# A four-layer graph network on one Trainium2 core: where ScalarE copies the spherical harmonics in the first layer's loop

## The chip, the cores and the metric

The kernel runs on one core of one Trainium2 chip. A core has five engines with a queue of instructions each: PE (TensorE, matmuls), DVE (VectorE), ACT (ScalarE), POOL (GpSimd) and SP (SyncE, which here only starts transfers). They wait for each other through semaphores. The metric is the device time of one execution in microseconds (us), the median of several runs.

## The reference, cut to what matters

A graph of 6250 nodes with 32 features and 200,000 edges goes through four layers, each after a layer norm and a ReLU, each added to its input. The change lies in the first, the harmonic layer: every edge takes the features of its source node, multiplies them with the 16 spherical harmonics of its direction, and the products are summed at the target node and multiplied with a weight matrix.

```
Y = real_sh_l3(edge_vectors)                              # [edges, 16]
msg = node_features[sources][:, :, None] * Y[:, None, :]
agg = jax.ops.segment_sum(msg, targets, num_segments=n_atoms)
out = agg.reshape(n_atoms, -1) @ W + b
```

The fourth layer needs `relu(e_feat @ en1_w.T + en1_b)` for every edge, 128 hidden units. The kernel computes these in the loop of the harmonic layer, too.

## The kernel before

Ahead of the layer the edges are sorted by target, into tiles of 128 edges that share a block of 128 target nodes. A table in HBM holds, for each node, its features already multiplied with the weights, 16 x 32 numbers a node (`harmonic_table`). So an edge's message is the sum over 16 products of a gathered row with its harmonics.

`harmonic_layer` (from L1088) walks over 404 chunks of four tiles (U = 4). A turn is Q = 4 chunks, there are 101 turns, and `each_turn` (L83) puts four turns into the body of a hardware loop and writes the rest out. Nearly every buffer exists four times, by q, the chunk's number in its turn; the harmonics in PSUM (`harm_ps`) and the edges turned over (`turned`) twice. `free`, `multiplied` and the other counters start with a lead, so that the first chunks don't wait. For chunk c:

- SP (L1127, L1128) loads the harmonics and the 32 edge features, once the sum of chunk c-4 is done (`free`). Both count on `loaded[q]`.
- POOL gathers 128 rows of 2 KB for each tile, four indirect transfers a chunk (`gather_all`, L1046), once the product of chunk c-4 is done (`multiplied`); every second chunk it copies the next indices (L1034).
- ACT, in this order: |iota - target| for four tiles, the first half of a one-hot (`one_hot_away`, L1070); a copy of the chunk's harmonics from SBUF to PSUM (L1149), after a wait for the product of chunk c-2 and one for the loads; the copy that lays the turned edge features flat in SBUF (L1151); the second half of the one-hot (L1076); then it waits for the hidden units on PE, writes their ReLU to SBUF (L1156) and starts the store to HBM (L1158).
- DVE: four products of gathered rows and harmonics, which it reads from PSUM (L1226), and one reduction over the 16 (L1232), which gives the message.
- PE, in this order: flip(c) turns the edge features over (L1175), sum(c-1) adds the messages of the chunk before at their targets with the one-hot as weights (L1194), hide(c) makes the hidden units (L1183), after the lay-flat copy of c.

An engine takes its instructions in order, so what stands behind a wait waits with it.

Of the kernel before, what the change touches and what calls it, by code (L numbers as in the profile page):

```python
# [8 lines left out]
ACT = mybir.ActivationFunctionType  # L9
# [6 lines left out]
NY = 16  # L16
# [3 lines left out]
U = 4  # L20
Q = 4
# [13 lines left out]
class Steps:  # L35
# [11 lines left out]
    def turn(self, i, each):  # L47

        return Steps(self.engine, self.sem, self.base + self.n + i * each)
# [33 lines left out]
def each_turn(engine, first, end, turn, join=JOIN):  # L83

    whole = (end - first) // join
    if whole:
        with engine.Fori(0, whole) as j:
            for x in range(join):
                turn(j * join + (first + x))
    for i in range(first + whole * join, end):  # L90
        turn(i)
# [49 lines left out]
def layernorm_root(k, act, small, squares_summed, scaled):  # L141

    act.wait_ge(squares_summed, 1)
    k.nc.scalar.activation(small[:, 1, :], small[:, 1, :], ACT.Sqrt).then_inc(scaled, 1)
# [922 lines left out]
def one_hot_away(k, s, c, hot, near):  # L1067

    for u in range(U):
        last = k.nc.scalar.activation(hot[:, u, :], k.iota[:, :], ACT.Abs, bias=k.neglo[s][:, bass.ds(c * U + u, 1)])  # L1070
    last.then_inc(near, 1)


def one_hot_of(k, hot):

    return k.nc.scalar.activation(hot[:, :, :], hot[:, :, :], ACT.Relu, bias=1.0, scale=-1.0)  # L1076
# [11 lines left out]
def harmonic_layer(k):  # L1088


    nc, s = k.nc, 1
    with ExitStack() as ctx:
# [5 lines left out]
        harm = [sb(f"h_harm{q}", [P, U, NY]) for q in range(Q)]  # L1098
# [9 lines left out]
        harm_ps = [pb(f"h_harm_ps{h}", [P, 512]) for h in range(2)]  # L1108
# [3 lines left out]
        loaded = [sem(f"h_loaded{q}") for q in range(Q)]  # L1112
        stored = [sem(f"h_stored{q}") for q in range(Q)]
        near, made, flipped, flat = sem("h_near"), sem("h_made"), sem("h_flipped"), sem("h_flat")
        hidden_done, hidden_made, multiplied, msg_made = sem("h_hid_done"), sem("h_hid_made"), sem("h_multiplied"), sem("h_msg_made")
        spread, ones_set = sem("h_spread"), sem("h_ones_set")
# [4 lines left out]
        @block.sync  # L1121
        def _(sp):
            def turn(i):
                for q in range(Q):
                    c = i * Q + q
                    sp.wait_ge(free, c + 1)
                    sp.dma_start(harm[q][:, :, :], k.harm_dram.rearrange("p (t j) -> p t j", j=NY)[:, bass.ds(c * U, U), :]).then_inc(loaded[q], 16)  # L1127
                    sp.dma_start(attr[q][:, :, :], rows[:, bass.ds(c * U, U), W_A32:W_A32 + D]).then_inc(loaded[q], 16)  # L1128

            each_turn(sp, 0, k.TURNS, turn)  # L1130
# [5 lines left out]
        @block.scalar  # L1136
        def _(act):
            for q in range(Q):
                act.sem_inc(stored[q], 16)
            act.sem_inc(flat, 1)  # L1140
            act.sem_inc(hidden_made, 1)
            def turn(i):
                for q in range(Q):
                    c = i * Q + q
                    act.wait_ge(free, c + 1)
                    one_hot_away(k, s, c, hot[q], near)
                    act.wait_ge(multiplied, c + (Q - 1))
                    act.wait_ge(loaded[q], 32 * i + 32)
                    nc.scalar.activation(harm_ps[q % 2][:, 0:U * NY], harm[q][:, :, :].rearrange("p u j -> p (u j)"), ACT.Copy).then_inc(spread, 1)  # L1149
                    act.wait_ge(flipped, c + 1)  # L1150
                    nc.scalar.activation(turned[q % 2][0:D, :], turned_ps[:, :], ACT.Copy).then_inc(flat, 1)  # L1151
                    act.wait_ge(near, c + 1)
                    one_hot_of(k, hot[q]).then_inc(made, 1)
                    act.wait_ge(hidden_done, c + 1)
                    act.wait_ge(stored[q], 16 * i + 16)
                    nc.scalar.activation(hidden[q][:, :], hidden_ps[:, :], ACT.Relu).then_inc(hidden_made, 1)  # L1156
                    act.wait_ge(hidden_made, c + 2)
                    act.dma_start(k.hid_dram[:, bass.ds(c * (U * EH), U * EH)], hidden[q][:, :]).then_inc(stored[q], 16)  # L1158

            each_turn(act, 0, k.TURNS, turn)  # L1160
            for q in range(Q):
                act.wait_ge(stored[q], 16 * (k.TURNS + 1))
            layernorm_root(k, act, small, squares_summed, scaled)
# [1303 lines left out]
```

## Time and profile before

| | us |
|---|---|
| median of 3 runs | 29608.59 |
| lowest and highest | 29582.97, 29622.8 |
| span of the profiled execution (no other time of it is shown) | 29570.9 |
| of it, from 5395 to 7779: the loop of the harmonic layer | 2384 |
| DVE busy with the products (L1226) | 1002.5 |
| DVE busy with the reductions (L1232) | 923.6 |
| ACT busy with the copies of the harmonics (L1149) | 82.6 |

The span runs from the first instruction to the last of one profiled execution. Busy time is what the instructions of a group took together; idle time before them is listed with the instruction that ended it. Matmuls are pipelined, and their ends are modelled. The fourth layer takes nearly half of the span and is not touched.

### The profile page before, as it was taken

What the parts mean: (1) busy time and instruction counts of PE and PEld (TensorE: products, weight loads), DVE (VectorE), ACT (ScalarE), POOL (GpSimd) and SP (SyncE); (2) the same over time, 40 slices, a digit from 0 to 9 for tenths busy, and PEclk for the clock granted to TensorE, in tenths of its full rate; (3) what the DMA queues carried; (4) which work ended last, traced back from release to release, by engine and by line L of the source; (5) the groups of instructions that cost most, each with busy time, mean ns of one, the idle gap of its engine ahead of it and who ended that gap; (6) DMA issues with size and microseconds to landing.
All of it is one profiled execution on the core that took longest, in us unless ns stands there. A gap on an engine that the chain in (4) does not pass through costs nothing. (4 is left out here: it accounts for less than half of the span.)

```text
span 29570.9 us, 552018 instructions
## 1 busy us (share of the span) xinstructions
PE 19304.6 (65%) x125786; PEld 16885.8 (57%) x125787; DVE 14123.3 (48%) x37141; ACT 10123.7 (34%) x24027; POOL 19962.3 (68%) x21448
## 2 busy tenths in 40 slices
PE   0000610788766677733333499899899899899899
PEld 0000300566422277633333389899899899899898
DVE  7700321688788855422222244444444444444444
ACT  0000000355333354333333344444344444344444
POOL 0776775466566677577777677677677677677676
PEclk9999755555699966655555599999899999999999
DMA  2114114788411144311211222222222222222222
GB/s 95 31 29 32 27 29 101 224 240 240 130 25 25 26 125 125 93 26 26 26 26 26 34 71 67 62 70 67 62 69 67 63 69 67 64 68 66 65 69 60
DMA packets 3128329, 2133.91 MB, mean 72 GB/s; under 512 B 2037459, under 2 KB 2626549, under 8 KB 3116567
## 3 DMA queue, kind: packets, MB, share of 16 engines
q1 hardware_dynamic: 2279528, 1072.10, 15.8%
q0 software_dynamic: 736448, 837.95, 12.4%
q10 hardware_dynamic: 109680, 190.99, 1.7%
q8 instruction: 1339, 21.94, 0.3%
q14 instruction: 1334, 10.93, 0.1%
HBM read 1679.95 MB, written 419.35 MB: 71 GB/s over the span
## 5 line engine op out<-in xcount | busy, mean ns | idle before, releaser
L2057 POOL DMA_INDIRECT e_got<-round_table,e_ring x9384 | 8984.7, 957 | 3690.5 <-issue 3047.8
L2278 DVE SCALAR_TENSOR_TENSOR e_spread<-e_ring,e_nodes,e_got 128x128 f32 x18816 | 5561.1, 352 | 6145.2 <-PE e_outer_ps L2177 3385.4
L2177 PE MATMUL e_outer_ps<-e_ring,e_spread 128*128 x37632 | 5530.2, 292 | 1153.8 <-issue 664.6
L2177 PEld LDWEIGHTS e_outer_ps<-e_ring,e_spread 128*128 128x128 f32 x37632 | 4843.2, 201 | 1273.6 <-issue 1273.6
L2085 ACT ACTIVATE e_outer<-e_outer_ps 128x516 f32<-128x516 f32 x4704 | 2824.1, 600 | 7278.5 <-PE e_outer_ps L2177 7144.6
L2198 PE MATMUL e_sum_ps<-w,e_turned 128*128 128x32 f32 x37632 | 4550.8, 273 | 0.0
L2198 PEld LDWEIGHTS e_sum_ps<-w,e_turned 128*128 128x128 f32 x37632 | 4476.2, 193 | 115.9 <-issue 115.9
L1046 POOL DMA_INDIRECT g_got<-second_table,g_index x3232 | 3082.5, 954 | 931.5 <-issue 741.0
L1871 PE MATMUL g_sums<-g_load,g_hot 128*128 128x64 f32 x6464 | 1566.4, 424 | 2562.1 <-DVEq L1903 2541.2
L1871 PEld LDWEIGHTS g_sums<-g_load,g_hot 128*128 128x128 f32 x6464 | 1438.6, 327 | 2689.8 <-issue 2668.5
L2188 PE MATMUL e_turn_ps<-ident,e_outer 128*128 128x128 f32 x18816 | 2926.6, 280 | 0.0
L2096 ACT ACTIVATE e_turned<-e_turn_ps 128x512 f32<-128x512 f32 x4704 | 2786.2, 592 | 33.0 <-PE e_turn_ps L2188 25.7
L2188 PEld LDWEIGHTS e_turn_ps<-ident,e_outer 128*128 128x128 f32 x18816 | 2307.5, 146 | 0.0
L1357 PE MATMUL m_spread<-m_diag,m_hot 128*128 128x512 f32 x3232 | 1666.7, 642 | 806.5 <-DVE m_diag L1373 806.4
L1046 POOL DMA_INDIRECT m_got<-near_table,m_index x1616 | 1529.3, 946 | 863.3 <-issue 583.0
L1046 POOL DMA_INDIRECT h_got<-harmonic_table,h_index x1616 | 1532.0, 948 | 783.6 <-issue 439.0
L740 POOL DMA_INDIRECT edges_by_src<-s_rows,s_to x1563 | 1600.8, 1024 | 610.6 <-issue 473.2
L1500 POOL DMA_INDIRECT edges_by_node<-a_inner x1616 | 1552.3, 961 | 531.0 <-issue 462.6
L1070 ACT ACTIVATE g_hot<-iota,neglo 128x128 f32<-128x128 f32 x3232 | 1031.3, 389 | 2482.8 <-PE g_sums L1871 2480.8
L740 POOL DMA_INDIRECT edges_by_dst<-s_rows,s_to x1563 | 1500.7, 960 | 486.7 <-issue 474.2
L765 ACT ACTIVATE s_rows<-words 128x44 f32 (+2 forms) x286 | 68.3, 239 | 4759.5 <-DMA edges_by_src<-s_rows,s_to 2124.3
L1357 PEld LDWEIGHTS m_spread<-m_diag,m_hot 128*128 128x128 f32 x3232 | 577.9, 198 | 1894.6 <-DVE m_diag L1373 1452.1
(393 smaller groups left out, 22752.2 us busy)
## 6 DMA issues: line engine op xcount, KB each, us to landing
e_ring<-edges_by_node SPq DMA_DIRECT2D x2346, 272.0 KB
e_got<-round_table,e_ring POOLq DMA_INDIRECT x9384
edge_hidden<-h_hidden ACTq DMA_DIRECT2D x404, 256.0 KB, 3.8
a_inner<-edge_hidden SPq DMA_DIRECT2D x404, 256.0 KB
g_got<-second_table,g_index POOLq DMA_INDIRECT x3232, 2.4
s_rows<-edge_attr SPq DMA_DIRECT2D x284, 176.0 KB, 2.7
edges_by_src<-pad ACTq DMA_DIRECT2D x16, 2020.0 KB, 35.0
edges_by_dst<-pad ACTq DMA_DIRECT2D x16, 2020.0 KB, 51.4
```

The source lines that it names most:

```text
L740: g.indirect_dma_start(k.edges[s], bass.IndirectOffsetOnAxis(ap=to[h][0:parts, u:u + 1], axis=0), rows[h][0:parts, u, :], None).then_inc(s ...
L1046: g.indirect_dma_start(into[q][:, u, :], None, table, bass.IndirectOffsetOnAxis(ap=index[q // 2][:, at:at + 1], axis=0)).then_inc(landed[q ...
L1357: last = nc.tensor.matmul(spread_ps[h][:, u, :], hot[q][:, h * HALF + u, :], diag[q % 2 * PAIRS + h][:, u, :, :].rearrange("p h e -> p (h ...
L1500: g_.indirect_dma_start(k.fine_rows, bass.IndirectOffsetOnAxis(ap=to, axis=0), inner[q][:, u, :], None).then_inc(scattered[q], 16)
L1871: last = nc.tensor.matmul(sums[q % 2][:, u * W:(u + 1) * W], hot[q][:, u, :], load[q][:, u, :], start=True, stop=True)
L2057: g_.indirect_dma_start(got[:, u, :], None, k.round_table, bass.IndirectOffsetOnAxis(ap=index, axis=0)).then_inc(landed[q], 16)
L2085: a_.activation(outer[h][:, at:at + U, :], outer_ps[:, n % 2 * 1024:(n % 2 + 1) * 1024].rearrange("p (x f) -> p x f", x=U)[:, :, 0:FULL], ...
L2096: a_.activation(turned[h][:, :, at:at + U * NEAR], turn_ps[:, n % 2 * 512:(n % 2 + 1) * 512].rearrange("p (x i) -> p i x", i=D), ACT.Copy) ...
L2177: last = t_.matmul(outer_ps[:, to:to + FULL], spread[n % 4][:, x, :], ring[:, bass.ds(at[x], 1), 0:FULL].rearrange("p a f -> p (a f)"), st ...
L2188: last = t_.transpose(turn_ps[:, to:to + P], outer[h][:, n % EACH * U + x, 0:P], k.ident[:, :])
L2198: t_.matmul(msg_ps, turned[h][:, i, :], k.w2[:, i * D:(i + 1) * D], start=i == 0, stop=False)
L2278: last = v.scalar_tensor_tensor(spread[n % 4][:, x, :].rearrange("p (j i) -> p j i", j=NEAR), ends.unsqueeze(2).to_broadcast(wide), nodes[ ...
```

## The change

ScalarE copies the harmonics one chunk ahead: those of chunk 0 before the loop, those of chunk c+1 between the second half of the one-hot of c and the wait for the hidden units of c. The two waits of the copy move with it. The number of copies and the buffers are the same. The last turn is written out on its own, because its last chunk has no next one.

```diff
-            def turn(i):
+
+            def show_harmonics(i, q):
+
+                act.wait_ge(multiplied, i * Q + (q + Q - 1))
+                act.wait_ge(loaded[q], 32 * i + 32)
+                nc.scalar.activation(harm_ps[q % 2][:, 0:U * NY], harm[q][:, :, :].rearrange("p u j -> p (u j)"), ACT.Copy).then_inc(spread, 1)
+
+            def turn(i, last=False):
                 for q in range(Q):
                     c = i * Q + q
                     act.wait_ge(free, c + 1)
                     one_hot_away(k, s, c, hot[q], near)
-                    act.wait_ge(multiplied, c + (Q - 1))
-                    act.wait_ge(loaded[q], 32 * i + 32)
-                    nc.scalar.activation(harm_ps[q % 2][:, 0:U * NY], harm[q][:, :, :].rearrange("p u j -> p (u j)"), ACT.Copy).then_inc(spread, 1)
                     act.wait_ge(flipped, c + 1)
                     nc.scalar.activation(turned[q % 2][0:D, :], turned_ps[:, :], ACT.Copy).then_inc(flat, 1)
                     act.wait_ge(near, c + 1)
                     one_hot_of(k, hot[q]).then_inc(made, 1)
+                    if not (last and q == Q - 1):
+                        show_harmonics(*((i, q + 1) if q < Q - 1 else (i + 1, 0)))
                     act.wait_ge(hidden_done, c + 1)
                     act.wait_ge(stored[q], 16 * i + 16)
                     nc.scalar.activation(hidden[q][:, :], hidden_ps[:, :], ACT.Relu).then_inc(hidden_made, 1)
...
-            each_turn(act, 0, k.TURNS, turn)
+            show_harmonics(0, 0)
+            each_turn(act, 0, k.TURNS - 1, turn)
+            turn(k.TURNS - 1, last=True)
```

## Rows read from the trace of the kernel before

**Rows 1.** Windows: start:end, length, busy us of each engine, clock, DMA share, GB/s

```profile
5395.00:7779.00 2384.00, 1971.09 (x8078) 1608.54 (x8077) 1923.76 (x2019) 1216.80 (x3227) 1571.58 (x1818) 0.50 0.83 239
5402.00:5452.00 50.00, 38.18 (x158) 31.59 (x159) 40.78 (x45) 23.52 (x63) 38.78 (x45) 0.51 0.89 263
7780.00:9000.00 1220.00, 805.02 (x1648) 296.74 (x1649) 1017.46 (x1698) 368.84 (x959) 743.42 (x865) 0.93 0.13 24
```

**Rows 2.** Waits, 5390 to 7790: who waited for whom, us, times, longest

```profile
ACT h_hidden L1156 <- PE h_hidden_ps L1183: 877.8, 404, 6.5
...
DVE h_product L1226 <- ACT h_harm_ps L1149: 438.3, 402, 6.3
PE h_sums L1194 <- DVE h_msg L1232: 397.4, 401, 5.8
...
DVE h_product L1226 <- DMA h_got<-harmonic_table,h_index: 9.1, 2, 8.0
```

**Rows 3.** Time line, two chunks: start, us, engine, line, operation, idle before

```profile
6511.23 2.48 DVE L1226 TENSOR_TENSOR h_product<-h_got,h_harm_ps 128x512 f32<-128x512 f32 x4 [0.63 <-ACT h_harm_ps L1149]
...
6513.75 2.29 DVE L1232 TENSOR_REDUCE h_msg<-h_product 128x128 f32<-128x2048 f32 x1
...
6516.18 1.91 PE L1194 MATMUL h_sums<-h_msg,h_hot 128*128 128x32 f32 x8 [0.56 <-DVE h_msg L1232]
...
6517.12 0.20 ACT L1149 ACTIVATE h_harm_ps<-h_harm 128x64 f32<-128x64 f32 x1
6517.27 0.57 ACT L1151 ACTIVATE h_turned<-h_turned_ps 32x512 f32<-32x512 f32 x1
6517.46 2.48 DVE L1226 TENSOR_TENSOR h_product<-h_got,h_harm_ps 128x512 f32<-128x512 f32 x4 [1.43 <-ACT h_harm_ps L1149]
6517.75 0.61 ACT L1076 ACTIVATE h_hot<-h_hot 128x512 f32<-128x512 f32 x1
...
6518.02 2.07 PE L1183 MATMUL h_hidden_ps<-en,h_turned 33*128 33x128 f32 x8
...
6518.79 0.38 SPq L1128 DMA_DIRECT2D h_attr<-edges_by_dst  x1
...
6520.02 1.03 PE L1175 MATMUL h_turned_ps<-ident,h_attr 128*32 128x128 f32 x4
6520.13 0.60 ACT L1156 ACTIVATE h_hidden<-h_hidden_ps 128x512 f32<-128x512 f32 x1 [1.77 <-PE h_hidden_ps L1183]
...
6521.38 1.28 ACT L1070 ACTIVATE h_hot<-iota,neglo 128x128 f32<-128x128 f32 x4 [0.65 <-ACT h_hidden L1156]
...
6522.56 0.20 ACT L1149 ACTIVATE h_harm_ps<-h_harm 128x64 f32<-128x64 f32 x1
...
6522.89 2.48 DVE L1226 TENSOR_TENSOR h_product<-h_got,h_harm_ps 128x512 f32<-128x512 f32 x4 [0.63 <-ACT h_harm_ps L1149]
```

**Rows 4.** Tile h_harm_ps: count, ns min/median/max, first and last start

```profile
L1226 DVE TENSOR_TENSOR h_product<-h_got,h_harm_ps x1616: 678/681/690, 5402.0 to 7778.4; 128x512 f32<-128x512 f32 x180
L1149 ACT ACTIVATE h_harm_ps<-h_harm x404: 202/204/228, 5395.8 to 7776.3; 128x64 f32<-128x64 f32 x135
```

**Rows 5.** Time line at a turn of ScalarE's loop

```profile
6715.86 1.28 ACT L1070 ACTIVATE h_hot<-iota,neglo 128x128 f32<-128x128 f32 x4 [1.05 <-issue]
...
6717.19 0.57 ACT L1151 ACTIVATE h_turned<-h_turned_ps 32x512 f32<-32x512 f32 x1
...
6717.81 2.07 PE L1183 MATMUL h_hidden_ps<-en,h_turned 33*128 33x128 f32 x8 [0.20 <-ACT h_turned L1151]
...
6720.01 0.60 ACT L1156 ACTIVATE h_hidden<-h_hidden_ps 128x512 f32<-128x512 f32 x1 [1.73 <-PE h_hidden_ps L1183]
```

**Rows 6.** Groups of POOL, 5390 to 7790: busy us, mean ns, idle before

```profile
L1046 POOL DMA_INDIRECT h_got<-harmonic_table,h_index x1616 | 1532.0, 948 | 783.6 <-issue 439.0 <-DVE h_product L1226 291.5 <-DMA h_got<-harmonic_table,h_index 50.3
L1034 POOL COPY h_index<-other 128x8 int32 (+1 forms) x203 | 40.8, 201 | 50.4 <-POOLq L965 36.1 <-issue 13.9
```

**Rows 7.** Tile h_attr, from issue to landing

```profile
DMA to landing us min/median/max: 2.7/3.7/11.7
```

## The prediction

> **What bounds the kernel now.** The page puts the harmonic layer in one stretch of 2384 us, and only this stretch is touched. I read its engine shares first, then who waits for whom, then the time line of two chunks, and last the engines' own work as floors.
>
> In the stretch no engine is full: PE is busy 1971 us (83%), DVE 1924 (81%), POOL 1572 (66%, without the time between its instructions), ACT 1217 (51%), and the 16 DMA engines 83%; PE runs at a granted clock of 0.50, that is 1.2 GHz [rows 1]. So the stage is bound by a round of waits, not by an engine. The waits say which: DVE's product waits for ScalarE's copy of the harmonics in 402 of 404 chunks, 438 us in all; PE's summing waits 397 us for DVE's message; ScalarE waits 878 us for the hidden units on PE [rows 2]. These three make one circle. The copy of the harmonics needs nothing of PE, but in ScalarE's program it stands behind the wait for the hidden units of the chunk before.
>
> The time line shows one lap [rows 3]. Call the chunk whose product starts at 6511.23 n. Product to reduction 2.52 us (6511.23 to 6513.75), the reduction 2.29, then 0.14 until PE starts to sum n (6516.18). From there: 1.84 to hide(n+1) at 6518.02, 2.11 to ScalarE's ReLU of it at 6520.13, 1.25 to the one-hot's first half for n+2 (6521.38; in it lie the ReLU's 0.60 and the issue of its store), 1.18 to the copy of the harmonics of n+2 (6522.56), and 0.33 to the product of n+2 (6522.89). Together 2.52 + 2.29 + 0.14 + 1.84 + 2.11 + 1.25 + 1.18 + 0.33 = 11.66 us for two chunks, which is what lies between the two products. Chunk n+1 (product at 6517.46) runs the same lap, shifted. So the steady period is **5.83 us a chunk**. The mean over the layer is (7776.3 - 5395.8)/403 = 5.91 [rows 4]; the 0.08 between them are the opening, a few late transfers, and ScalarE's loop turn every 16 chunks, whose gap before the one-hot is 1.05 in place of 0.65 [rows 5]. These I leave as they are.
>
> **The change part by part.**
>
> 1. The copy of chunk c+1 now stands in front of the wait for hide(c). Number and size of the copies are the same: 404 of 0.20 us, so added work is nothing, and each moves past no DMA of its own queue except the store of the hidden units, which it now precedes. ScalarE gets there with time to spare: between the one-hot's second half (6517.75 + 0.61 = 6518.36) and the ReLU (6520.13) it sits idle 1.77 us [rows 3], and the copy takes 0.20 of them. That is its cover. In the new pace below the same gap is 1.7 us, so it stays covered; without that cover it would cost up to 0.20 x 404 = 81 us. The last lap's circle is opened: the product of c+1 no longer hangs on hide(c).
>
> 2. Between the one-hot's first half and the lay-flat copy the harmonics are gone: 6517.12 to 6517.27, 0.15 us a chunk [rows 3].
>
> 3. Two waits come forward with the copy: for product(c-1), which frees the PSUM bank, and for the loads of chunk c+1. Behind them on ScalarE stand the ReLU, its store and the next one-hot, and PE waits for those. What they cost in the new pace is worked out below: nothing, with room.
>
> 4. The first copy ahead of the loop waits for a load that the old code waited for as well; the gather of chunk 0 sets the first product at 5402.0 [rows 4], long after the copy. Nothing. The last turn was written out before too (101 turns are 25 times 4 and one), so there is no code more to load.
>
> **What is late next.** With this circle open, each remaining one has a period of its own, and the longest sets the pace:
>
> - ScalarE and PE: hide(c), ReLU(c), one-hot(c+1), lay-flat(c+1), hide(c+1). When PE really waits for the lay-flat copy, as it does once at a loop turn, hide starts 0.62 after the copy's start (6717.19 to 6717.81) and the ReLU starts 2.20 after hide (6720.01) [rows 5]. With 1.25 and 1.18 from [rows 3] that is 2.20 + 1.25 + 1.18 + 0.62 = **5.25 us**. With the 2.11 of an unhindered PE it would be 5.16.
> - POOL: its 1616 gathers are busy 1532.0, idle 783.6, of which 291.5 only for DVE's product, and its index copies take 40.8 plus the 14 of issue before them: (1532.0 + 783.6 - 291.5 + 40.8 + 14)/404 = 5.15 at most [rows 6].
> - DVE: 2.52 + 2.29 = 4.81, some 0.1 more to start the next product.
> - PE alone: summing 1.84, hide 2.00 (6518.02 to 6520.02), flip 1.03: 4.87 [rows 3].
> - DMA: 0.83 of 2384/404 = 5.90 is 4.90 us a chunk at a share of one [rows 1].
>
> I take 5.25, because it is the longest and comes from a place where exactly this wait was the last. Is nothing else in its way? Count from the start of hide(c) as t. The second half of the one-hot ends at about t + 0.45, the copy for c+1 runs to t + 0.65, and the ReLU is due at t + 2.20. Product(c+1) can start at t + 0.8, product(c) a period earlier, so its reduction ends near t + 0.4; PE wants it after the flip, at t + 3.0. Product(c-1) ended still earlier, so the wait for the bank costs nothing. The loads of c+1 are issued when sum(c-3) ends, just ahead of hide(c-2), at t - 10.5; the second is issued 0.8 later (6518.79 against 6518.02 [rows 3]) and lands in 3.7 (median), at t - 6.0; even the slowest, 11.7 [rows 7], is there at t + 2.0, ahead of the ReLU. POOL starts the gather for c+4 when product(c) has ended and has over 10 us until it is needed.
>
> **The sum.** (5.83 - 5.25) x 404 = 234 us less in the layer. The page shows no time of this execution beside its span of 29570.9 us; the span is 38 us under the median of the runs, 29608.6, and that goes with both kernels. 29608.6 - 234 = **29375 us**, 0.8% less. The bounds of this case: at 5.16 it would be 271 us less, 29338; with 5.35 (the three floors at 4.9 to 5.15 meeting the ring at bad moments, a tenth of a microsecond a chunk) 194 less, 29415.
>
> **The rivals.**
>
> - **The DMA engines become the bound.** 4.90 us of work in a period of 5.25 is a share of 0.93. What the trace has held in this layer over 50 us is 0.89 at 263 GB/s, in its opening [rows 1]. If 0.89 is the most, the period is 4.90/0.89 = 5.51 and the gain 0.32 x 404 = 129: 29480. For it: no row shows 0.93. Against it: nothing says that 0.89 was the most they could do. 12%.
> - **PE's clock rises.** The row shows 0.50 through the layer with PE busy 83%, while the stretch 7780 to 9000 has 0.93 with PE busy only 66% [rows 1]. PE would go from 83% to 4.87/5.25 = 93% busy. If that brings 2.4 GHz, hide halves and the ScalarE ring falls by about 1 us; POOL's 5.15 is then the bound: 0.68 x 404 = 275 less, 29334, or 29310 if POOL's issue gaps shrink too. By the two rows busy share alone does not decide, so 6%.
> The Trainium skill, page "TensorE: Matmul & The Clock Gate", section "What's actually happening", says that the ratio follows how busy PE has been, half when idle and full once busy; by that rule this rival would be the likely one, and by it the layer should already be at the full clock, which the row contradicts.
> - **The wait moves and nothing is won.** The product then waits for its gather instead. Against it: POOL waited 291.5 us for the product, so it is ahead [rows 6], and the gather is named twice, with 9 us, as what the product waited for [rows 2]. It would need POOL at 5.8 a chunk. 29590 to 29610, 4%.
> - **Slower: a late load now holds up ScalarE.** The wait for the loads of c+1 stands in front of ReLU(c). The circle sum(c-3), load (0.8 + L), copy 0.2, ReLU to one-hot 1.25, 1.18, 0.62 to hide(c+1) spans three chunks. It passes the old pace when (0.8 + L + 0.2 + 3.05)/3 is over 5.83, that is from a landing time L of 13.4 us on. With L = 15 the period is 6.35 and the time 0.52 x 404 = 210 more, 29819. For it: fuller DMA queues make loads late, and the longest landing is 11.7. Against it: the median is 3.7 [rows 7], under a third of what it takes. 3%.
>
> **How the numbers follow.** My case 75%, the four rivals 12, 6, 4 and 3%. Some 0.2% (59 us) is what a measurement of this kernel can tell from no change; the three runs shown lie within 40 us. My case, the DMA's and the clock's are all faster by more than that; I take a little off for a wait that I have not seen: faster 0.90, same 0.07, slower 0.03. The range runs from the clock's lower end, 29310, to the DMA's, 29480.
>
> **What would show each step.** After the change the product's wait for the copy of the harmonics is nearly gone, and so is most of the sum's wait for the message; PE's wait for the lay-flat copy, seen before at a loop turn, stands at nearly every chunk with 0.3 to 0.4 us; the layer lasts about 2150 us; copies start at a spacing of 5.25 and stand between the one-hot's second half and the ReLU; the granted clock stays 0.50; the DMA share is 0.92 or so. Right for the DMA rival: landings of gathers above their present ones and POOL or the product waiting on them. Wrong altogether: the product waits for a gather, or ScalarE idles in front of the copy.

## The result and the profile after

| | before | after |
|---|---|---|
| median, us | 29597.46 (4 runs) | 29349.47 (4 runs) |
| lowest to highest | 29582.97 to 29622.8 | 29324.32 to 29391.83 |
| ratio, 95% interval | | 0.9914 (0.99 to 0.9928) |
| span of the profiled execution | 29570.9 | 29390.0 |
| layer, first to last copy of the harmonics | 2380.5 | 2119.3 |

248 us less, where 234 were forecast (29375 from the median shown then); the measured time lies in the range. The layer alone gave 261. The two spans differ by only 181: the profiled execution after is the slowest of its four (29391.83), and its last layer, which no edit touches, took 46 us more than in the profile of before (transposes from 16630.1 to 29326.7 against 16868.9 to 29519.3). The harmonic layer also began later there (first copy at 5405.6 against 5395.8), so its last sum starts 250 us earlier (7532.9 against 7783.1) and not 261. So I judge the variants below by the layer's time in the profile, and take the totals beside it.

The line numbers behind the edit are 8 higher after: the product is L1234, the reduction L1240, the sum L1202, hide L1191, the ReLU L1162, the lay-flat copy L1155; the copy of the harmonics is L1147. The copies and products of after, in the view of the tile harm_ps (counterpart of [rows 4]):

```profile
L1234 DVE TENSOR_TENSOR h_product<-h_got,h_harm_ps x1616: 676/680/690, 5410.5 to 7528.1; 128x512 f32<-128x512 f32 x180
L1147 ACT ACTIVATE h_harm_ps<-h_harm x404: 200/200/230, 5405.6 to 7524.9; 128x64 f32<-128x64 f32 x135
```

(7524.9 - 5405.6)/403 = 5.26 us a chunk in place of 5.91. The waits of after, 5390 to 7790, counterpart of [rows 2]:

```profile
ACT h_hidden L1162 <- PE h_hidden_ps L1191: 626.0, 400, 6.3
...
PE h_hidden_ps L1191 <- ACT h_turned L1155: 257.8, 402, 1.3
...
DVE h_product L1234 <- ACT h_harm_ps L1147: 177.3, 384, 7.5
...
ACT h_harm_ps L1147 <- DMA h_attr<-edges_by_dst: 44.3, 6, 25.6
```

The sum's wait for the message, 397 us before, is no longer among the large ones (6.9 us in the view of groups). In its place PE waits for the lay-flat copy before hide in 402 of 404 chunks. Of ScalarE's 44.3 us of waits for loads 25.6 lie ahead of the first copy, at the layer's start; the other five come from 7485 on, in the last chunks.

One chunk of after in the time line, counterpart of [rows 3]:

```profile
6506.74 0.60 ACT L1162 ACTIVATE h_hidden<-h_hidden_ps 128x512 f32<-128x512 f32 x1 [1.53 <-PE h_hidden_ps L1191]
...
6507.98 1.28 ACT L1070 ACTIVATE h_hot<-iota,neglo 128x128 f32<-128x128 f32 x4 [0.65 <-ACT h_hidden L1162]
...
6509.17 0.57 ACT L1155 ACTIVATE h_turned<-h_turned_ps 32x512 f32<-32x512 f32 x1
...
6509.65 0.61 ACT L1076 ACTIVATE h_hot<-h_hot 128x512 f32<-128x512 f32 x1
...
6509.79 2.07 PE L1191 MATMUL h_hidden_ps<-en,h_turned 33*128 33x128 f32 x8 [0.58 <-ACT h_turned L1155]
...
6510.17 0.20 ACT L1147 ACTIVATE h_harm_ps<-h_harm 128x64 f32<-128x64 f32 x1
6510.50 2.48 DVE L1234 TENSOR_TENSOR h_product<-h_got,h_harm_ps 128x512 f32<-128x512 f32 x4 [0.36 <-ACT h_harm_ps L1147]
...
6511.90 0.60 ACT L1162 ACTIVATE h_hidden<-h_hidden_ps 128x512 f32<-128x512 f32 x1 [1.54 <-PE h_hidden_ps L1191]
```

This is the ring of the prediction: ReLU to one-hot 1.24, to the lay-flat copy 1.19, to hide 0.62, to the next ReLU 2.11, together 5.16 (6506.74 to 6511.90). The copy stands in ScalarE's idle time ahead of the ReLU.

Not every lap is like this one. The rows below are the ReLU of a turn's last chunk, the one-hot and the ReLU of the next turn's first chunk, and the ReLU of its second:

```profile
6517.07 0.60 ACT L1162 ACTIVATE h_hidden<-h_hidden_ps 128x512 f32<-128x512 f32 x1 [1.53 <-PE h_hidden_ps L1191]
...
6518.39 1.28 ACT L1070 ACTIVATE h_hot<-iota,neglo 128x128 f32<-128x128 f32 x4 [0.72 <-ACT h_hidden L1162]
...
6522.39 0.60 ACT L1162 ACTIVATE h_hidden<-h_hidden_ps 128x512 f32<-128x512 f32 x1 [1.62 <-PE h_hidden_ps L1191]
...
6527.56 0.60 ACT L1162 ACTIVATE h_hidden<-h_hidden_ps 128x512 f32<-128x512 f32 x1 [1.53 <-PE h_hidden_ps L1191]
```

The lap into a new turn takes 5.32: ReLU to one-hot is 1.32 in it, and from hide, which starts at 6520.20, to the ReLU are 2.19. The next lap takes 5.17. Over the whole layer it is the same: three of four laps are 5.16 or 5.17, the fourth is 5.32, and where ScalarE's loop turns back it is 5.66. The mean from chunk 16 to chunk 384 is 5.225 us (ReLUs at 5498.37 and 7421.16); before, it was 5.870 (5499.02 and 7659.21). The windows, in the columns of [rows 1]:

```profile
5500.00:7500.00 2000.00, 1745.82 (x7622) 1534.15 (x7621) 1814.02 (x1904) 1134.77 (x3050) 1494.03 (x1722) 0.50 0.91 269
```

The DMA engines moved 269 GB/s at a share of 0.91, and PE's granted clock stayed 0.50 (1.2 GHz) with PE busy 87%.

### The profile page after: what moved, and what is told of

The parts are those of the page before. It is cut to its first block and busy times, and to the rows that moved or that the text cites. A ratio compares the mean times of both kernels' runs of the same rounds, so it can differ in the third digit from the quotient of the medians.

```text
span 29390.0 us, 552043 instructions
## 1 busy us (share of the span) xinstructions
PE 19266.7 (66%) x125786; PEld 16981.7 (58%) x125787; DVE 14114.1 (48%) x37141; ACT 10110.1 (34%) x24027; POOL 20002.1 (68%) x21448
```

## The experiments

All variants are edits of the changed kernel; diffs are against it. The layer's time is from the first to the last copy of the harmonics.

| | layer, us | median, us | ratio to before (95%) |
|---|---|---|---|
| before | 2380.5 | 29597.46 | 1 |
| the change | 2119.3 | 29349.47 | 0.9914 (0.99 to 0.9928) |
| the change again | 2125.2 | 29377.09 | 0.9918 (0.9901 to 0.9934) |
| copy in the ring | 2179.9 | 29406.15 | 0.9933 (0.9916 to 0.995) |
| copy behind the ReLU | 2197.4 | 29433.17 | 0.994 (0.9924 to 0.9957) |
| one-hot ahead, copy not | 2156.3 | 29384.08 | 0.9925 (0.9908 to 0.9941) |
| second copy, covered | 2212.9 | 29452.53 | 0.9948 (0.9932 to 0.9965) |
| second copy, short loop | 2128.9 | 29397.4 | 0.9923 (0.9906 to 0.9939) |
| more DMA | 2132.3 | 29389.35 | 0.9917 (0.99 to 0.9934) |
| no copy | 2218.3 (products) | 29488.94 | 0.995 (0.9933 to 0.9966) |
| both ahead | 2063.9 | 29288.27 | 0.9894 (0.9877 to 0.991) |
| both ahead, again | 2068.6 | 29296.66 | 0.9893 (0.9877 to 0.991) |

The kernel before, run beside them, had a median of 29600 us for the copy in the ring, the copy behind the ReLU, the covered second copy and both ahead; 29631 for the change again, the short loop, more DMA and no copy; 29607 for the other two.

### The change again

No edit.

> The changed kernel again, as it stands beside its variants on one chip. If the layer's time is what its ring makes it, it is again 5.16 us a chunk in the steady stretches and 2115 to 2125 us from first to last copy of the harmonics, whatever the total does; the total differs by what the rest of the kernel does, some 29320 to 29390.

The layer took 2125.2 us, at the upper edge of what was expected; the total fell by 29630.64 - 29377.09 = 254 us. Two profiles of one kernel differ by 6 us in this layer, so a difference of 15 in it can be read, and in the totals one of some 50.

### The copy in the ring

```diff
                     one_hot_away(k, s, c, hot[q], near)
+                    if not (last and q == Q - 1):
+                        show_harmonics(*((i, q + 1) if q < Q - 1 else (i + 1, 0)))
                     act.wait_ge(flipped, c + 1)
...
                     one_hot_of(k, hot[q]).then_inc(made, 1)
-                    if not (last and q == Q - 1):
-                        show_harmonics(*((i, q + 1) if q < Q - 1 else (i + 1, 0)))
```

> The copy is still one chunk ahead, but stands between the one-hot's first half and the lay-flat copy. My theory: the pace is now set by the ring hide, ReLU, one-hot's first half, lay-flat copy, hide (5.16 us a chunk in the changed kernel), so whatever stands in it counts: 5.31 us a chunk, the layer from first to last copy of the harmonics 2119 + 60 = 2180 us, the kernel 60 us slower than the changed one, some 190 faster than before. Rival: only the long circle through product, sum and hide mattered, and it is as open here as there: 5.16 and 2119 us.

2179.9 us, what the ring makes: 0.15 us a chunk more in it are 60 us of layer. That it agrees to the microsecond is luck, as two profiles of one kernel differ by 6. The rival's 2119 is ten times that away, and falls.

### The copy behind the ReLU

```diff
                     one_hot_of(k, hot[q]).then_inc(made, 1)
-                    if not (last and q == Q - 1):
-                        show_harmonics(*((i, q + 1) if q < Q - 1 else (i + 1, 0)))
...
                     act.dma_start(k.hid_dram[:, bass.ds(c * (U * EH), U * EH)], hidden[q][:, :]).then_inc(stored[q], 16)
+                    if not (last and q == Q - 1):
+                        show_harmonics(*((i, q + 1) if q < Q - 1 else (i + 1, 0)))
```

> The copy of the next chunk stands behind the wait for the hidden units, the ReLU and its store, but ahead of the next one-hot. My theory: the long circle is closed again but without the one-hot's 1.18 us, (2.52+2.29+0.14+1.84+2.11+1.25+0.33)/2 = 5.24 us a chunk, and the ring with the copy in it takes 5.31, which decides: layer 2180 us, like the copy in the ring. Rival: what cost was the copy's place behind the wait for PE as such, then it goes back to the 5.83 of before, layer 2380 us.

2197.4 us, 17 over the forecast and far from the 2380 of the rival. The time line of this variant shows where most of the 17 come from:

```profile
6504.07 0.60 ACT L1160 ACTIVATE h_hidden<-h_hidden_ps 128x512 f32<-128x512 f32 x1 [1.64 <-PE h_hidden_ps L1191]
...
6505.35 0.23 ACT L1147 ACTIVATE h_harm_ps<-h_harm 128x64 f32<-128x64 f32 x1 [0.68 <-ACT h_hidden L1160]
6505.51 1.26 ACT L1070 ACTIVATE h_hot<-iota,neglo 128x128 f32<-128x128 f32 x4
...
6509.41 0.60 ACT L1160 ACTIVATE h_hidden<-h_hidden_ps 128x512 f32<-128x512 f32 x1 [1.64 <-PE h_hidden_ps L1191]
```

The lap is 5.34 (6504.07 to 6509.41), not 5.31, which makes 12: behind idle time a copy takes 0.23 us, not 0.20, and starts 1.28 after the ReLU, not 1.25. The product waited 255 us for the copy and the sum 120 for the message, so the long circle (5.24) and the ring (5.34) are near each other here.

### The one-hot ahead, the copy not

```diff
+            def start_hot(i, q):
+
+                act.wait_ge(free, i * Q + (q + 1))
+                one_hot_away(k, s, i * Q + q, hot[q], near)
...
                     c = i * Q + q
-                    act.wait_ge(free, c + 1)
-                    one_hot_away(k, s, c, hot[q], near)
+                    show_harmonics(i, q)
                     act.wait_ge(flipped, c + 1)
...
                     if not (last and q == Q - 1):
-                        show_harmonics(*((i, q + 1) if q < Q - 1 else (i + 1, 0)))
+                        ahead = (i, q + 1) if q < Q - 1 else (i + 1, 0)
+                        start_hot(*ahead)
...
-            show_harmonics(0, 0)
+            start_hot(0, 0)
```

> The copy of the harmonics stays where it was before, behind the wait for the hidden units and for its own chunk; only the one-hot's first half goes one chunk ahead, in front of that wait. My theory of the circle through product, sum, hide, ReLU and copy: the one-hot's 1.18 us leave it, (4.81+0.14+1.84+2.11+1.25+0.33)/2 = 5.24 us a chunk, while ScalarE's own ring (4.1 with the copy in it) doesn't bind: layer 5.24 x 403 + 35 = 2147 us from first to last copy, the product waiting for the copy nearly always. Rival: what matters is that the copy stands behind the wait for PE at all; then it stays near 5.83 and 2380 us.

2156.3 us, 9 over the forecast, and not 2380. Here the copy hangs on the wait for PE exactly as it did before, and yet six sevenths of the layer's gain are there: 224 of 261 us. What cost the kernel before was not the wait as such but the length of the circle that ran through it, of which the one-hot's 1.18 us were a part for nothing. One forecast was off: the product names the copy 208 times, not nearly always. The circle spans two chunks, and one of the two closes it: its product waits for the copy, and the other one's follows straight on DVE's own reduction. So products are spaced unevenly, but two by two they keep the circle's time: those that waited for the copy start at 6562.43, 6572.96 and 6583.49, 10.53 apart where 10.48 was forecast, with the copy about 1.28 behind the ReLU in place of 1.25. The mean from chunk 16 to 384 is 5.29, as here too the turns cost something on top. The two rows are the waits of this variant:

```profile
DVE h_product L1239 <- ACT h_harm_ps L1152: 214.0, 208, 9.0
PE h_sums L1207 <- DVE h_msg L1245: 187.0, 204, 5.9
```

### A second copy in ScalarE's idle time

```diff
                 act.wait_ge(loaded[q], 32 * i + 32)
+                nc.scalar.activation(harm_ps[q % 2][:, U * NY:2 * U * NY], harm[q][:, :, :].rearrange("p u j -> p (u j)"), ACT.Copy)
                 nc.scalar.activation(harm_ps[q % 2][:, 0:U * NY], harm[q][:, :, :].rearrange("p u j -> p (u j)"), ACT.Copy).then_inc(spread, 1)
```

> A second copy of the harmonics, into unused columns of the same PSUM bank, just ahead of the first. My theory: ScalarE has 1.5 us of idle time in front of its ReLU, so 0.15 to 0.20 us more there cost nothing: 5.16 us a chunk, layer 2119 us. Rival: ScalarE's own work, or DVE's wait for the copy (still 177 us), is part of the pace: 60 to 80 us more.

2212.9 us: 94 more, which by the number alone would give the rival the point. The rows don't. Ahead of the one-hot ScalarE idled 107.5 us in 24 places where nothing released it; in the kernel before it was 25 us in 24. The three views are the wait, the time line at one such place, and a line of the list of DMA queues between 5500 and 7400 (packets, MB, share):

```profile
ACT h_hot L1070 <- issue: 107.5, 24, 5.7
```

```profile
6543.62 0.34 ACTq L1165 DMA_DIRECT2D edge_hidden<-h_hidden  x1
6549.03 1.28 ACT L1070 ACTIVATE h_hot<-iota,neglo 128x128 f32<-128x128 f32 x4 [5.58 <-issue]
```

```profile
q14 instruction: 108, 0.88, 0.2%
```

24 is the number of times ScalarE's loop turns back, and a queue that loads instructions is busy in the layer, which it is not in the changed kernel. There are 16 copies more in the body of four turns, and the body seems no longer to stay loaded: where the loop turns back, the idle time ahead of the one-hot is 4.5 us on average (107.5/24) in place of 1.05, and the lap is 9.09 in place of 5.66. That is 3.4 us more in each of 24 laps, 82 of the 94 us. Away from the loop's turns the lap with the second copy is 5.16 as before (ReLUs at 6532.54 and 6537.70). The Trainium skill, page "Runtime: NRT & Kernel Launch", section "Instruction fetch mechanics", says that an engine keeps only a small window of instructions and that a taken branch to a place outside it must fetch first. These rows agree; the price, 3.4 us a lap, is this run's.

So the copy itself was tried again with half the body:

```diff
+                nc.scalar.activation(harm_ps[q % 2][:, U * NY:2 * U * NY], harm[q][:, :, :].rearrange("p u j -> p (u j)"), ACT.Copy)
...
-            each_turn(act, 0, k.TURNS - 1, turn)
+            each_turn(act, 0, k.TURNS - 1, turn, 2)
```

> The second covered copy again, with ScalarE's loop body two turns long in place of four. Where the second copy stood in the long body, the layer took 94 us more, and 82 of these stand at the 24 loop turns, where ScalarE idles 4 to 5.6 us and instructions are loaded again. My theory: the copy itself is covered and the body had grown past what stays loaded: with half the body the instruction transfers in the layer are gone, a loop turn costs 0.4 us again but comes 50 times, the layer is 2125 to 2140 us. Rival: the copy's own 0.15 us is not covered: 2180 us or more also with the short body.

2128.9 us. No instruction transfers in the layer, 49 turns with 51.7 us of idle time in all:

```profile
ACT h_hot L1070 <- issue: 51.7, 49, 1.1
```

10 us over the change (4 over its second run) are no more than 25 more loop turns at 0.4 us make; the copies themselves cost nothing that can be read, where uncovered ones would cost some 60. ScalarE's idle time covers them.

### More work for the DMA engines

```diff
+        spare = [sb(f"h_spare{q}", [P, U, D]) for q in range(Q)]
...
                     sp.dma_start(attr[q][:, :, :], rows[:, bass.ds(c * U, U), W_A32:W_A32 + D]).then_inc(loaded[q], 16)
+                    sp.dma_start(spare[q][:, :, :], rows[:, bass.ds(c * U, U), W_A32:W_A32 + D]).then_inc(loaded[q], 16)
...
-                act.wait_ge(loaded[q], 32 * i + 32)
+                act.wait_ge(loaded[q], 48 * i + 48)
...
-                pe.wait_ge(loaded[q], 32 * i + 32)
+                pe.wait_ge(loaded[q], 48 * i + 48)
```

> Every chunk's edge features are loaded a second time, into spare buffers that nobody reads, and the waits for the loads wait for these too. The loads of harmonics and features took about a tenth of the DMA engines' time before, 0.63 us a chunk, most of it the features with their 128-byte rows. It makes the DMA work of a chunk 4.70 + 0.5 = 5.2 us at a share of one. If the DMA engines can be nearly full, the pace is 5.3 to 5.4 us and the layer 2140 to 2200 us; if 0.91 is about their ceiling, as the DMA rival has it, 5.7 us and 2300 us, with the product or ScalarE's copy waiting for transfers. If the work is hidden, 2119 us.

2132.3 us. In the steady stretch the pace is 5.17 (products at 6504.35 and 6509.52), with the DMA engines at 0.96 and 283 GB/s:

```profile
5500.00:7400.00 1900.00, 1666.30 (x7271) 1465.66 (x7272) 1731.41 (x1819) 1082.01 (x2907) 1420.79 (x1642) 0.50 0.96 283
```

The load is hidden, the third of the outcomes. The engines' share rose by 0.05 only, 0.26 us a chunk where 0.5 was estimated, but not because the load is cheaper: in the list of DMA queues between 5500 and 7400 the queue of the loads went from 11.6% to 21.1%, which is the 0.5, while the gathers' queue fell from 65.9% to 61.3% for the same 383 MB. So the share that a transfer takes is not a fixed price, and a floor that is worked out from it, like the 4.90 us of the prediction, is a loose one. A ceiling at 0.89 or 0.91 there is not; where one lies above 0.96 was not tried.

Most of the 13 us over the change (7 over its second run) come from the layer's last chunks; the mean from chunk 16 to 384 is 5.229 us, the change's own. There a load is late in each of the three kernels; this is ScalarE's longest wait for one, in this variant, in the change and in the kernel before:

```profile
7500.06 0.23 ACT L1149 ACTIVATE h_harm_ps<-h_harm 128x64 f32<-128x64 f32 x1 [18.46 <-DMA h_spare<-edges_by_dst]
```

```profile
7498.11 0.23 ACT L1147 ACTIVATE h_harm_ps<-h_harm 128x64 f32<-128x64 f32 x1 [8.65 <-DMA h_attr<-edges_by_dst]
```

```profile
7749.20 0.23 ACT L1149 ACTIVATE h_harm_ps<-h_harm 128x64 f32<-128x64 f32 x1 [5.59 <-DMA h_attr<-edges_by_dst]
```

From 7450 to 7500 the changed kernel's DMA engines moved 217 GB/s at a share of 0.91, in place of 269: the same busy time carries less. It is my rival of the late loads, real in a handful of chunks and dearer the sooner the copy is due. Why the transfers are slow there was not tried.

### No copy

```diff
-                        show_harmonics(*((i, q + 1) if q < Q - 1 else (i + 1, 0)))
+                        pass
...
-            show_harmonics(0, 0)
...
-                    dve.wait_ge(spread, c + 1)
+                    dve.wait_ge(loaded[q], 32 * i + 32)
...
-                                               harm_ps[q % 2][:, u * NY:(u + 1) * NY].unsqueeze(1).to_broadcast([P, D, NY]), ALU.mult)
+                                               harm[q][:, u, :].unsqueeze(1).to_broadcast([P, D, NY]), ALU.mult)
```

> No copy of the harmonics at all: DVE reads them from SBUF and waits for their load itself. It opens the long circle as the change does, and leaves ScalarE's ring as it is in the changed kernel: 5.16 us a chunk, layer 2119 us, if a product with its small operand in SBUF takes the 0.68 us that it takes from PSUM. No row shows that duration: from 0.75 us on DVE (4 products and 2.29) is the bound, and at 0.8 it makes 5.6 us a chunk and 2260 us. Rival: DVE's late start (177 us of waits for the copy) is part of the pace of the changed kernel, then the layer falls below 2119.

The product took 0.684 us, as from PSUM, and still the layer is 101 us slower than with the copy: products from 5405.0 to 7623.3, 2218.3 us, where the change has 2117.6. Neither theory had this. The groups of POOL between 5500 and 7400, first of the change, then of this variant:

```profile
L1046 POOL DMA_INDIRECT h_got<-harmonic_table,h_index x1462 | 1390.4, 951 | 471.7 <-issue 404.2 <-DMA h_got<-harmonic_table,h_index 49.7 <-POOL h_index L1034 8.8
L1034 POOL COPY h_index<-other 128x8 int32 x182 | 36.6, 201 | 2.1 <-issue 1.5
```

```profile
L1046 POOL DMA_INDIRECT h_got<-harmonic_table,h_index x1392 | 1424.7, 1024 | 399.3 <-issue 337.3 <-DMA h_got<-harmonic_table,h_index 48.7 <-POOL h_index L1034 13.3
L1034 POOL COPY h_index<-other 128x8 int32 x174 | 76.3, 438 | 0.4
```

The wait of this variant:

```profile
DVE h_product L1233 <- DMA h_got<-harmonic_table,h_index: 272.4, 316, 8.3
```

The gathers take 1.02 us on POOL in place of 0.95, the index copies 0.44 in place of 0.20, and now the product waits 272 us for its gathers: POOL is the bound. The only thing that changed for POOL is where DVE reads its small operand. The time line of this variant has the long ones under a product:

```profile
6503.46 2.52 DVE L1233 TENSOR_TENSOR h_product<-h_got,h_harm 128x512 f32<-128x512 f32 x4 [1.36 <-DMA h_got<-harmonic_table,h_index]
...
6504.40 0.42 POOL L1034 COPY h_index<-other 128x8 int32 x1
...
6504.98 1.25 POOL L1046 DMA_INDIRECT h_got<-harmonic_table,h_index  x1 [0.16 <-issue]
```

Not every gather under a product is long: those at 6509.04 and 6510.29, under the next product, took 0.95. The Trainium skill, page "SBUF — State Buffer", section "SBUF: two separate sides", says that a DVE instruction with two inputs in SBUF holds for its whole length a port that it shares with GpSimd, against a GpSimd instruction that reads SBUF. The measured rows agree in direction, but why some gathers escape they do not show. The copy to PSUM has a use that no row of the kernel before had shown.

### The one-hot and the copy ahead

```diff
+            def start_hot(i, q):
+
+                act.wait_ge(free, i * Q + (q + 1))
+                one_hot_away(k, s, i * Q + q, hot[q], near)
...
-                    act.wait_ge(free, c + 1)
-                    one_hot_away(k, s, c, hot[q], near)
                     act.wait_ge(flipped, c + 1)
...
                     if not (last and q == Q - 1):
-                        show_harmonics(*((i, q + 1) if q < Q - 1 else (i + 1, 0)))
+                        ahead = (i, q + 1) if q < Q - 1 else (i + 1, 0)
+                        show_harmonics(*ahead)
+                        start_hot(*ahead)
...
+            start_hot(0, 0)
             show_harmonics(0, 0)
```

> The one-hot's first half for the next chunk goes ahead of the wait for the hidden units too, behind the copy. My theory: the ring falls from 5.16 to 2.11+1.25+0.62 = 3.98 us, and the next floor sets the pace, POOL's 5.05 to 5.15 us of gathers and index copies a chunk: layer 2040 to 2080 us, the kernel 20 to 60 us faster than the changed one; the product then waits for its gather, and PE no more for the lay-flat copy. Rival: the DMA engines, at 0.91 in the changed kernel, are already as full as they get: 5.16, layer 2119 us, with longer landings of the gathers.

2063.9 us and 29288 in all, 61 under the change. PE's wait for the lay-flat copy is gone, and what remains is POOL, which waited only 18 us for the product in the whole layer, in 60 places; the waits and the window:

```profile
DVE h_product L1240 <- DMA h_got<-harmonic_table,h_index: 143.8, 204, 8.8
PE h_sums L1208 <- DVE h_msg L1246: 125.5, 171, 6.7
```

```profile
5500.00:7400.00 1900.00, 1803.72 (x7498) 1494.12 (x7498) 1774.38 (x1876) 1131.42 (x3000) 1459.83 (x1687) 0.50 0.92 278
```

The pace is (7464.9 - 5401.0)/403 = 5.12 us, and 5.07 from chunk 16 to 384, at POOL's floor (5.05 to 5.15 by my reckoning). Run again:

> One-hot and copy both ahead, again, beside the run above on one chip: layer 2064 us within 5 us from first to last copy, with POOL's gathers as the bound; the kernel 280 to 340 us faster than before, and some 60 to 90 faster than the one with the one-hot alone ahead.

2068.6 us, a ratio of 0.9893, and 29384.08 - 29296.66 = 87 us under the one-hot alone ahead on the same chip. This version beats both kernels.

## Why the prediction was right

**The circle that bound the kernel before** was right, and so were its parts. With the one-hot alone taken out of it, the layer moved as the sum of the parts says (2156 against a forecast of 2147). With the copy ahead of the one-hot it came to 2197 against 2180; there the ring is the longer, so that run shows that the circle is no longer than 5.34, and not its sum.

**The cover of the moved copy** was right: 0 us, shown with the second copy in the short loop.

**What is late next** was right: ScalarE and PE's ring. Its size was off by 0.09 us in three of four chunks. I took 2.20 from hide to ReLU from the one place at which PE waited for the lay-flat copy, and laid it down to that wait. It belongs to something else: in both kernels the step is 2.20 in the first chunk of a turn of four (99 of 101 turns before, 98 after) and 2.11 in the others. The place that I had read was the start of a turn [rows 5].

The sum came out near for a reason that is partly luck. I set one lap of 5.83 against one of 5.25. The means between chunks 16 and 384 are 5.870 and 5.225: (5.870 - 5.225) x 404 = 261, as measured, where the bound of 5.16 would give (5.83 - 5.16) x 404 = 271. The turns account for the 10 between them. In the kernel before, going into a new turn adds some 0.09 to the circle; in the change it adds 0.16 to the ring, because the one-hot's later start (1.32 for 1.25) and the late ReLU (2.20 for 2.11) both lie in it. So the turns, which I left as they were, cost 0.04 a chunk before and 0.06 after, and 5.25, which hardly a lap has, is close to the mean of all. What in a turn's first chunk makes these steps longer, I did not trace.

**The waits moved forward** cost nothing in the steady stretch, as reckoned: between 5450 and 7400 ScalarE waited for no load. In the last chunks they cost some microseconds, in the way that the slower rival describes: after its first copy ScalarE waited five times for a load, 18.7 us in all, where before it waited 6.9 in two.

**Two statements were wrong.** The first: that the product's wait for the copy would be nearly gone. It is 177 us in 384 chunks. My own times say so: DVE needs 4.81 us of 5.16 and must wait 0.35 for something, and the copy, which ScalarE reaches some 0.4 us after hide starts, is what comes last. By the ring's sum this wait costs nothing: 177 us could vanish and the ring would still be 5.16.

The second: that PE would wait 0.3 to 0.4 us for the lay-flat copy in each chunk. It waits 257.8/402 = 0.64. I had added up PE's own work from the kernel before, 1.84 + 2.00 + 1.03 = 4.87. In the change the sum no longer waits for the message: it starts 0.82 behind the flip and takes 1.75, so with hide PE needs 2.00 + 0.82 + 1.75 = 4.57. This is no part of the ring either.

**The rivals.** The DMA rival priced a share of 0.89 as a ceiling; the change ran at 0.91 and the variant at 0.96 without loss. The clock stayed at 0.50, with PE busy 87% in the change and 95% with both ahead, so this rival did not come. The rule of the Trainium skill, page "TensorE: Matmul & The Clock Gate", section "What's actually happening", that a busy PE gets the full clock, does not hold for these stretches. The late loads came in a handful of chunks, where the rival needed all of them.

## What to carry to other kernels

Where one engine waits for another in every chunk, follow the lap until it closes and add up the parts: each microsecond of work of that engine that stands behind the wait and needs nothing from it belongs in front of it. Which piece moves first matters less than how much leaves the circle; then reckon the next ring, and move the next piece out of that. Count the loop body's instructions when something is added to it, and where the idle time "issue" at loop turns grows, look in the list of DMA queues for instruction transfers. And before a lap of a pipelined loop is taken as the pace, look at several, across the body's repeats: here every fourth one is longer.

## What the runs showed of the hardware

- With 16 copies more in the body of ScalarE's loop, the engine idled 4.5 us ahead of the one-hot, where the loop turns back, in place of 1.05, with 108 packets of instruction transfers in 1900 us where the changed kernel has none.
- With both operands of DVE's product in SBUF in place of one in PSUM, DVE took the same 0.68 us, but POOL's index copies went from 0.20 to 0.44 us and its gathers from 0.95 to 1.02.
- DMA engines at a mean share of 0.96 (283 GB/s, 383 of 538 MB of it gathered rows) did not slow a loop that leads its loads by four chunks (5.229 us a chunk in place of 5.225), and the gathers' share fell from 65.9% to 61.3% for the same bytes when other loads were added.
- PE stayed at 1.2 GHz (granted clock 0.50) with a busy share of 0.95 over 1900 us.
